# Loads of q moved to ScalarE's queue, the SyncE queue reordered in seven units, and the value product put last in each key block

## The reference, cut to what matters

```python
x: [8, 1024, 256]                       # 8 batches of 1024 tokens
xn = layernorm(x)                       # eps 1e-5, no weights
# attention: 16 q heads, 8 kv heads, head dim 16; each kv head serves 2 q heads
energy = q @ k.T + alibi                # alibi = -|i - j| * 2^-(head + 1)
attn   = softmax(energy / 4)
y_attn = (attn @ v).reshape(...) @ Wo.T + bo
# feed-forward: one linear layer on a quantised input
s      = max(amax(|xn|), 1e-6) / 127    # one scale for each token
xq     = clip(round(xn / s), -128, 127)
y_lin  = (xq @ weight_q.T) * s * weight_scale + bias
out    = x + y_attn + y_lin
```

## Time and profile before

| | us |
|---|---|
| median of 3 runs | 1568.98 (1568.5 to 1569.91) |
| the profiled execution | 1568.38, span 1566.4 |
| PE busy | 1497.0 (96%) |
| DVE busy | 1394.6 (89%) |
| ACT busy | 1184.8 (76%) |
| POOL busy | 1076.1 (69%) |
| chain that ended last | PE 47%, DVE 30%, SP's queue 9%, issue 8%, DMA 3% |

### The profile page before, as it was taken

One profiled execution on the slowest core, in us unless ns is written; L12 is line 12 of the kernel. 1 busy time (PEld: TensorE's weight loads), 2 busy tenths in 40 slices (PEclk: granted clock), 3 DMA queues, 4 the chain that ended last, 5 costly groups with the idle time before them and its releaser, 6 DMA issues.

```text
span 1566.4 us, 42517 instructions
## 1 busy us (share of the span) xinstructions
PE 1497.0 (96%) x16284; PEld 583.0 (37%) x16284; DVE 1394.6 (89%) x1698; ACT 1184.8 (76%) x2331; POOL 1076.1 (69%) x1627
## 2 busy tenths in 40 slices
PE   5899999999999999999989999999999999999998
PEld 5333333333333333333333334333333333333333
DVE  5999989999899998999979999899998988999981
ACT  3467777777787776887767887777877777788885
POOL 5467777777788876787757877677877776533332
PEclk9999999999999999999999999999999999999999
DMA  6522243333334334333333433433333332312212
GB/s 169 140 76 71 74 100 81 93 98 81 105 83 108 96 79 109 91 92 101 84 92 94 105 85 91 103 98 96 97 83 96 94 92 65 82 49 68 72 44 62
DMA packets 197291, 140.98 MB, mean 90 GB/s; under 512 B 107040, under 2 KB 165728, under 8 KB 197088
## 3 DMA queue, kind: packets, MB, share of 16 engines
q1 hardware_dynamic: 197088, 138.27, 34.2%
HBM read 81.40 MB, written 35.63 MB: 75 GB/s over the span
## 4 chain that ended last, share of the span: by engine, by line
PE 47%; DVE 30%; SPq 9%; issue 8%; DMA 3%; POOL 2%; ACT 0%; POOLq 0%; DVEq 0%; ACTq 0%
DVE row_max L999 27%; PE ps_ring L1279 15%; PE ps_pv L1355 13%; PE ps_row L1296 9%; PE ps_ring L1395 4%; PE ps_ring L1415 3%; SPq L464 2%; SPq L468 2%; SPq L506 2%; DMA q<-neg_max_t 1%; SPq L472 1%; PE ps_ring L1398 1%; DMA k<-k_alibi 1%; DVE pv_turned L1039 1%; PE ps_ring L1409 1%
## 5 line engine op out<-in xcount | busy, mean ns | idle before, releaser
L999 DVE TENSOR_REDUCE row_max<-ps_row 128x1 f32<-128x1024 f32 x1024 | 1199.5, 1213 | 114.7 <-PE ps_row L1298 99.4
L1171 ACT ACTIVATE probs<-ps_ring 128x512 f32<-128x512 f32 x2048 | 1084.5, 601 | 245.2 <-PE ps_ring L1279 242.6
L1279 PE MATMUL ps_ring<-q,k 122*32 122x512 bf16 x8192 | 636.6, 383 | 19.9 <-DMA q<-neg_max_t 19.0
L762 POOL TENSOR_TENSOR probs<-probs,near 128x256 f32<-128x256 f32 x512 | 375.2, 733 | 324.8 <-ACT probs L1171 318.9
L1355 PE MATMUL ps_pv<-probs,v_unit 128*32 128x512 f32 x4096 | 533.5, 596 | 0.0
L1279 PEld LDWEIGHTS ps_ring<-q,k 122*32 122x32 bf16 x8192 | 215.1, 95 | 518.0 <-ACT probs L1171 324.7
L1296 PE MATMUL ps_row<-k,q 64*128 64x512 bf16 x944 | 326.2, 385 | 25.8 <-DVE row_max L999 11.4
L1298 PE MATMUL ps_row<-k_again,q_again 64*128 64x512 bf16 x944 | 326.0, 385 | 0.0
L1296 PEld LDWEIGHTS ps_row<-k,q 64*128 64x128 bf16 x944 | 84.2, 93 | 320.3 <-issue 199.6
L1355 PEld LDWEIGHTS ps_pv<-probs,v_unit 128*32 128x32 f32 x4096 | 124.7, 110 | 54.2 <-issue 7.7
L1298 PEld LDWEIGHTS ps_row<-k_again,q_again 64*128 64x128 bf16 x944 | 84.0, 92 | 0.0
(11 more groups left out here) (84 smaller groups left out, 1012.0 us busy)
## 6 DMA issues: line engine op xcount, KB each, us to landing
parts_dram<-parts SPq DMA_DIRECT2D x59, 288.0 KB, 3.0
q_again<-q SPq DMA_DIRECT2D x63, 256.0 KB, 3.3
token_b<-token_dram SPq DMA_DIRECT2D x53, 256.0 KB, 4.1
q<-parts_dram SPq DMA_DIRECT2D x128, 96.0 KB
k<-parts_dram SPq DMA_DIRECT2D x256, 32.0 KB
q<-parts_dram SPq DMA_DIRECT2D x128, 64.0 KB
att_dram<-att_unit SPq DMA_DIRECT2D x126, 64.0 KB
att_t<-att_dram SPq DMA_DIRECT2D x56, 128.0 KB, 2.9
```

Source lines behind the costliest of these rows:

```text
L762: pool.tensor_tensor(here, here, near[:, u % KV_HEADS, :].rearrange("p (e n) -> p e n", e=GROUP), ALU.mult).then_inc(weighted, 1)
L999: dve.tensor_reduce(row_max[:, par, e, qb:qb + 1], ps_row[qb % 2][:, :], AX_X, ALU.max, negate=True).then_inc(row_max_found, 1)
L1171: act.activation(probs[:, c % PBUFS, e, h * HALF:(h + 1) * HALF], ring_bank(u, c, e, h), ACT.Exp, scale=SCALE).then_inc(ring_freed, 1)
L1279: mm = pe.matmul(to[at, :], weights[:, at], moving, start=start, stop=stop)
```

## The change

Six edits are made.

1. The loads of a set are factored into `load_rows` and `load_q`. For sets 0, 1 and 2, ACT issues the loads of q, behind `find_middle(10)` and ahead of the first `keep_v`; SP issues those of k, and everything from set 3 on.
2. In the prologue the tiles 0 to 7 run first, then 8 to 10. On DVE the row maxima of the first 8 tiles leave the loop and stand behind it, ahead of `normalise(8)`.
3. In the units that hold the copy of a late set, SP issues `load_token`, `load_again`, `place_max`, `store_att` and `load_att_t` ahead of `next_set`.
4. In even units DVE sums the previous unit's rows after its maximum 7 (was 5), and turns its product back after 11 (was 13); POOL's `norm` of it stands at the start of block 4 (was at the end of block 3).
5. In units 0 and 1 DVE's work on the two tiles is split between blocks 1 and 3 (was all in block 1).
6. On PE `pv_block` stands after both column scores of the second head (was between them); the last batch's projections stand in pairs in every second block.

```diff
+        def load_q(eng, u, slot):
+            g, tok, pairs = u % KV_HEADS, (u // KV_HEADS) * SEQ, KV_HEADS // (QK_CHUNKS - 1)
+            for e in range(GROUP):
+                load_rows(eng, q_set[:, slot, e, :], g // pairs, tok, (g % pairs * GROUP + e) * HEAD_DIM, "q",
+                          first_rows_loaded if u == 0 and e == 0 else set_loaded[slot])
...
+                if u >= SETS - 1:
+                    load_q(sp, u, slot)
...
-                if u + 2 < UNITS and late_set(u + 2):
+                copied = u + 2 < UNITS and late_set(u + 2)
+                if copied:
+                    if f["token"]:
+                        load_token(u + 1 + PREP_AHEAD)
                     load_again(u + 2, (u + 2) % SETS)
+                    place_max(u + 1, (u + 1) % SETS)
+                    store_att(u - 1)
+                    for t in f["next_att"]:
+                        load_att_t(t, t % 2)
                 if f["row_set"] and not late_set(u + 3):
                     next_set(u + 3)
...
-            for t in range(PREP_AHEAD):
-                if t + 2 < PREP_AHEAD:
+            for t in range(BLOCKS):
+                if t + 2 < BLOCKS:
                     normalise(t + 2, t % 2)
...
+            for t in range(BLOCKS, BLOCKS + 2):
+                first_stats(t)
+            for t in range(BLOCKS):
+                find_first_largest(t)
+            find_first_scales(0, BLOCKS, 0)
+            for t in range(BLOCKS, BLOCKS + 2):
+                normalise(t, t % 2)
+            first_stats(PREP_AHEAD - 1)
+            find_rest(BLOCKS, 0, early[0][1])
+            normalise(PREP_AHEAD - 1, 0)
...
-                at_sums, at_norm = (5, BLOCKS) if apart else (3, 3)
+                at_sums, at_norm = (BLOCKS - 1, SLOTS) if apart else (3, 3)
+                made = 1 if u < PAIR else PAIR
...
-                        if i == SLOTS - 3 and apart:
+                        if i == BLOCKS + 3 and apart:
                             turn_back(u - 1)
-                    if c == 1:
-                        for t in f["normed"]:
+                    if c in (1, 3):
+                        for t in f["normed"][here(c)]:
...
+            for i in range(FIRST_PARTS):
+                act.wait_ge(first_parts_stored[i], 16 * len(range(i, BLOCKS, FIRST_PARTS)))
+            for u in range(SETS - 1):
+                load_q(act, u, u)
...
+                    project_pairs(u, c)
                     col_half(u, c, 1, 0)
+                    col_half(u, c, 1, 1)
                     if c >= 2:
                         pv_block(u, u % 2, c - 2)
                     elif f["prev"]:
                         pv_block(u - 1, (u - 1) % 2, BLOCKS - 2 + c)
-                    col_half(u, c, 1, 1)
```

## The result

The changed kernel takes 1608.79 us (median of 4 runs, 1607.36 to 1612.57), the kernel before 1568.74 beside it: ratio 1.0266, 95% interval 1.0236 to 1.0295. It is slower by 40 us; 15 were forecast and the range ended at 1594. The profiled execution took 1609.69, span 1606.7.

What follows compares the result with a forecast made beforehand. PE, 96% busy, was taken as the bound, with small mutual engine waits and stalls at batch ends. 1568.38 + 10.5 + 6 - 2 - 0.3 + 1 = 1583.6, with the median 0.6 above the profiled execution: 1584 us, range 1557 to 1594.

Steps and rivals of the forecast that it cites:

- Key blocks: PE's key blocks in the 64 units: moving the value product changes nothing, 0 us (-3 to +4).
- Units 0 and 1: First two units: spreading DVE's tile work, where PE waited and the clock fell, saves 2 us (-3.5 to +0.5).
- Prologue: Before unit 0: late tiles and q loads on ACT delay its start by 10.5 us (+4 to +14).
- 11.3 us, and I take 11.5 with the waits ahead of them: Prologue, ACT's queue: issuing 18 q loads, reckoned from SP's 1.88 us per triple, takes 11.5 us.
- Batch ends: Units around each late set: old stalls go, new ones come at units 8k, net +6 us (-12 to +12).
- the stall of 4.4 us with its upper bound of 4.8: Start of units 8, 16, ..., 48: PE waits 4.4 us for the negated maxima, between 1.5 and 4.8.
- The clock: Batch ends: lower PE clock behind the new stalls costs about 2.4 us in total.
- clock drops behind stalls of over 3 us, as 3 of the 7 stalls before had: Batch ends: stalls over 3 us bring clock drops, about 2.4 us, by the example of the kernel before.
- The rest: Other units and the end: paired projections -0.3 us and new order at unit ends +1, together +0.7.
- the +1 for the other units: Ends of the units: the new order of work there brings a step of 1 us.
- Rival B: Batch ends: old stalls vanish and none replace them, -23.8 us, total 1554 (1546 to 1560); chance 0.16.
- The 2.0 us that the prediction tried for the token store: Batch ends: with 2.0 us for this DMA, stalls would be 1.45 us, batch ends -12, the whole about 1566.

Runs made afterwards that it cites:

- e3: The kernel before with only the value product moved behind both column scores of the second head: 1568.18 us, ratio 0.9961.
- e5: The changed kernel with q loads of sets 0 to 2 back on SP, tiles in the new order: 1602.17 us, ratio 1.0200.
- e6: The changed kernel with the prologue's 11 tiles in one loop as before, q loads still on ACT: 1599.28 us, ratio 1.0185.
- e9: The changed kernel with SP's near_bias load moved behind set 2's k loads: 1611.73 us, one run.
- e7: The changed kernel with only set 0's q loads on ACT, those of sets 1 and 2 on SP: 1601.20 us, ratio 1.0207.
- e2: The changed kernel with place_max(8k) moved right behind the next set in units 8k-1: 1565.53 us, ratio 0.9952.
- e10: The changed kernel with SP's k loads of sets 1 and 2 right behind those of set 0: 1608.53 us, one run.
- e4: The kernel before with only SP's new order in units 8k-2, DVE's turned product as late as before: 1615.12 us, ratio 1.0256.
- e1: The changed kernel with SP's order in units 8k-2 put back as before: 1573.96 us, ratio 1.0019.

## Why the prediction was wrong

The mechanisms and their places were the forecast's; the sizes of the loads on ACT, of the new stalls and of the clock drops behind them were too small, and the sum left the range.

1. **Key blocks, 0: right.** Units 28 and 29 are unchanged, and e3 shows it for the edit alone.
2. **Units 0 and 1, -2: right** (-1.8). The mean clock of unit 1 is 1.00 instead of 0.94, as the term had it; kernels with edit 5 have 24.5 to 24.8 in unit 1, those without 26.2 to 26.6. The gain is not safe: in e5, e6 and e9 unit 0 takes 23.4 to 23.7 instead of 22.1, at a clock of 0.93, and -0.2 is left.
3. **Prologue, +10.5: mis-sized, +14.9.** The row scores (48.1 against 47.5) and what waits for `keep_v(0)` were as worked out. The failed step is "11.3 us, and I take 11.5 with the waits ahead of them" for ACT's 18 loads: they took 15.6, 4.1 more, since the last six were slow. SP's rows did not show that: the same 18 loads took SP 11.0, in triples of 1.81 to 1.88. Two more errors nearly cancel. The last split ended at 40.4, not 42, so `keep_v(0)` came 2.5 late (56.0 against 53.5) and not 4.1. Behind it the sum lets DVE go on at once with its 21 maxima, but the first of them starts at 58.83, 2.8 later: PE made a value product and the next row scores first, at a mean clock of 0.73 over 56 to 66. That makes up the 2 us which are still missing.

   e5, e6 and e7 add what the sum did not say: the two edits are dear only together. Against 68.2 to 72.1 with the prologue of before, unit 0 starts at 70.5 with the loads on ACT alone and at 74.4 with the tile order alone, but at 82.4 to 83.6 with both (five profiled runs), because the late tiles delay the loads and the loads delay `keep_v`.
4. **Batch ends, +6: mis-sized, +26.5.** The old stalls went, and new ones came one unit later, as forecast: `store_att` was put at 16.5 us and is at 16.67; `place_max(8k)` was put at 26.6 and is at 25.4 to 28.9 (20.5 in unit 55), 28.1 in unit 31. There the steps slipped one after another, against the forecast: next set 19.1 (18.5), its copy 31.3 (30), the odd unit's set 13.8 (12.4), `place_max` 28.1. The 1.5 us of the last one is what unit 31 is over the forecast (32.04 against 30.4). The failed step is the stall of 4.4 us with its upper bound of 4.8: PE stood idle for 3.97, 6.67, 5.43, 5.89, 6.29, 5.14 and 1.50 us, 34.9 together, and five of the seven are above the bound. The units 8k-1 are 37.5 us over their usual length, where 27.4 were taken; half of the difference to 34.9 is a wait of 1.29 us before row scores in unit 55, which the sum did not have.
5. **The clock, 2.4: the step that failed most in proportion.** The step "clock drops behind stalls of over 3 us, as 3 of the 7 stalls before had" was a misreading as well as too little: the three drops before stood behind stalls of 2.17, 3.23 and 4.29 us, and one of 2.98 had none. The longer stalls brought a drop in six of seven cases, and the units behind them lost 1.35 to 2.8 each, 12.7 together. Unit 32 shows that it is the clock: a mean of 0.90 over 22.44 us is about 4.5 us at the lower level (1.2 instead of 2.4 GHz), and half of that is its excess of 2.2. The account of the batch ends: 37.5 + 12.7 - 23.8 = 26.4, against 26.5 measured.
6. **The rest, +0.7: right by luck.** Unit 63 and the end take 34.0 instead of 33.2, as in all nine profiled kernels with the projections in pairs, where -0.3 was taken; and the +1 for the other units is not there.

Rival B (stalls that just vanish, 23.8 us) was wrong for the change, and one more move does not quite reach it: in e2 the batch ends are 16.3 below the kernel before, since small waits and a clock drop stay. The page of the Trainium skill (DMA: Bandwidth & Descriptors, "Issuing engines are not separate DMA queues") calls the issuing time usually small; here 18 issues held ACT 15.6 us, and by the measured number it was not. The 2.0 us that the prediction tried for the token store, from that page of the Trainium skill ("Anatomy of one DMA — SWDGE (gpsimd) path"), is given there for DMAs that GpSimd issues, while SP issues this one; the token DMAs between 838 and 856 us in the changed kernel took 3.3 to 5.0 us to land.

## What to carry to other kernels

When a wait is removed by moving a queue's entries, the entries it is moved past become late; follow the queue to the next unit's critical entry, and put that one ahead of everything that waits for a landing (e2: 43 us for one moved call). Slips along such a chain add up, so the range has to lean to the long side, and a stall of several us should be charged with the low clock behind it. Loads on a computing engine's queue cost that engine their issue time, with what it does next: put them behind the work that others wait for (e7: 6 loads there instead of 18, and unit 0 starts 8.4 us earlier).

## What was not expected of the hardware

A run of 18 loads on ACT's queue was issued at 0.68 us each for the first 12 and at 1.0 to 1.4 for the last six (48.24 to 55.67 in the changed kernel), in e9 and e10 too; SP issued the same 18 at 0.61 each in the kernel before. The clock fell behind each of the 13 longest stalls of the kernel before, the changed kernel and e4 (3.97 to 8.69 us), and not behind those of 1.5 and 0.3 us ahead of unit 56 in the latter two. Among shorter stalls the length alone does not decide: in e1 the clock fell behind 1.98 us (unit 15) and stayed up behind 3.38 us (unit 39).
